# Attention stage of a six-stage image model: ScalarE's functions and the feature split one step back

## The chip, the cores and the metric

One core of a Trainium2 chip. The metric is the device time of one execution in microseconds, from three runs: 6,864.52 median, 6,858.64 lowest, 6,875.67 highest.

## The reference

32 images of 16 x 16 tokens with 192 channels pass through six stages: a Mamba block, a Fourier block, a determinantal attention (the change is here), a gated mixture of experts, attention over a small memory, a second mixture of experts. The attention, for each token i of each of 12 heads with 16 channels:

```python
sim = k @ q_i; sim = where(arange(T) <= i, sim, -inf)
_, top_idx = top_k(sim, 8)                     # 8 nearest earlier keys
for comb in (8 singles, 28 pairs):             # together with token i itself
    K, V = k[idx], v[idx]
    log_det = log(det(K @ K.T) + 1e-6)         # score = log_det / (2 or 3)
    out_s = softmax(K @ q_i / 4) @ V
probs = softmax(scores); y = probs @ outs      # then a projection, added to x
```

## The kernel before, in words

`dpp_attention_phase` works through the 32 images in 12 steps each; a step is two heads of one half (128 tokens) of the image, steps 0 to 5 the first half (128 keys), steps 6 to 11 the second (256 keys, two one-hots, twice the gather). Each engine runs a hand-written `body(n, u, i, back, last)` per step, `steps` (L2076) lays them out: image 0, then a loop whose body holds two images (an odd one, then an even one), then image 31, then one empty pass that drains the pipeline. An engine executes its queue in order, so the order of the calls in `body` is the order of the work; semaphores join the engines.

The path of a step's index, for step i:

- PE computes the scores (`score`, L2647), one step ahead.
- VectorE finds the 8 largest and their positions (L2529, L2536).
- ScalarE casts the positions (`cast_index`, L2205), PE turns them (L2659), ScalarE copies the result (`copy_turned`, L2213), SyncE writes it to HBM (L2137) and reads it back spread over 128 partitions (L2143).
- VectorE makes the one-hot from it in step i+2 (L2544).
- PE gathers keys, values and norms with it in step i+3 (L2678); ScalarE evacuates the two halves (`take_gathered`, L2222 to L2224).
- GpSimd multiplies key pairs (`products`, L2333 to L2339) in its step i+3; VectorE sums them to dots in step i+4 (L2553).

The rest of an image n is done in the steps of image n+1, by constants: VectorE's sim stage in step 0 (L2395 to L2400), denominators in 1 (L2408, L2410), gaps in 3 (L2420 to L2430), determinants in 4 (L2438 to L2451), scores in 5 (L2460 to L2464), rows in 6 (L2473 to L2482), alpha in 7; GpSimd's weighing (L2322) in 7 and 8, VectorE's sum of it in 8 and 9. Between two such stages ScalarE has one function: `differences` (Exp, L2237, step 0), `denominators` (Ln, L2241, step 1), `gaps` (Square, L2245, step 3), `logs` (Ln, L2249, step 4), `weights` (Exp, L2254, step 5). Each waits for VectorE's stage of its own step, and VectorE's stage of a later step waits for it. Within ScalarE's body the order is: `take_gathered` twice, `cast_index`, the function, then the front of the next image (`normalise`, `front`), last `copy_turned`.

The gather's operand `feat3` is the image's features in three bf16 pieces: ScalarE rounds (`split_high`, L2194), GpSimd subtracts (`split_rest`, L2309), ScalarE rounds the rest (`split_middle`, L2198), GpSimd subtracts again (`split_low`, L2314). In the kernel before, the first two are issued in step 11 of the image before, the last two in step 0 of the image. `keep_own` (L2232) copies the token's own value.

Of the kernel before, what the change touches and what calls it, by code (L numbers as in the profile page):

```python
# [15 lines left out]
B, HH, WW, C = 32, 16, 16, 192  # L16
# [10 lines left out]
def counted(n):  # L27


    return n + 1  # L30
# [1965 lines left out]
def dpp_attention_phase(nc, x_res, moments, consts, w):  # L1996

    with ExitStack() as ctx:
# [95 lines left out]
                body(B, 0, i, back, True)  # L2094

        SIMS, DENOM, GAP, DET, SCORE, ROWS, ALPHA, VALUE, OUT, PROJECT = 0, 1, 3, 4, 5, 6, 7, 8, 10, 11
        FRONT, NORMALISE, SQUARE, OWN, SPLIT = 3, 2, 10, 11, 11

        def whole(n):

# [2 lines left out]
        def previous(n, u, i, k):  # L2103

            return (n - 1, 1 - u) if i == k and (whole(n) or n > 0) else None

        def next_image(n, u, last):

            return None if last or (isinstance(n, int) and n == B) else (n + 1, 1 - u)
# [11 lines left out]
        with nc.Block() as block:  # L2121
# [27 lines left out]
            def _(act):  # L2149
# [42 lines left out]
                def split_high(n, u):  # L2192
                    act.wait_ge(S["own_ready"], counted(n + 1))
                    nc.scalar.copy(feat3[:, u, :, 0, :, :], feat[:, u, :, :, :]).then_inc(S["mid_ready"], 1)  # L2194

                def split_middle(n, u):
                    act.wait_ge(S["rest_ready"], counted(n + 1))
                    nc.scalar.copy(feat3[:, u, :, 1, :, :], rest_f[:, :, :, :]).then_inc(S["mid_ready"], 1)  # L2198

                def cast_index(n, u, i):  # L2200

                    q = count_of((n, u, i))
                    act.wait_ge(S["found_ready"], q * 2 + 2)
                    act.wait_ge(S["turned"], counted(q - 1) if not (isinstance(q, int) and q < 2) else 1)
                    nc.scalar.copy(index[:, i % 2, :, :], found[:, i % 2, :, :]).then_inc(S["index_ready"], 1)  # L2205
# [56 lines left out]
                def body(n, u, i, back, last):  # L2262
                    real, s3 = not (isinstance(n, int) and n == B), back(3)
                    if s3:
                        take_gathered(s3, 0)
                        take_gathered(s3, 1)
                    if real:
                        cast_index(n, u, i)
                    for k, do in ((SIMS, differences), (DENOM, denominators), (GAP, gaps), (DET, logs),
                                  (SCORE, weights), (OUT, out)):  # L2270
                        if previous(n, u, i, k):
                            do(*previous(n, u, i, k))
                    if i == 1 and not (isinstance(n, int) and n == B):
                        keep_own(n, u)
                    nxt = next_image(n, u, last)
                    if nxt and i == NORMALISE:
                        normalise(nc, xn[:, :, :], x_res, rstd, shift, nxt[0] * 2).then_inc(S["xn_ready"], 1)
                    if nxt and FRONT <= i < FRONT + 8:
                        front(*nxt, i - FRONT)
                    if nxt and i == SPLIT:  # L2280
                        split_high(*nxt)
                    if i == 0 and real:
                        split_middle(n, u)
                    if real:
                        copy_turned(n, u, i)

                normalise(nc, xn[:, :, :], x_res, rstd, shift, 0).then_inc(S["xn_ready"], 1)
                for k in range(8):
                    front(0, 0, k)
                split_high(0, 0)  # L2290
                steps(act, body)

            @block.gpsimd
            def _(pool):
# [12 lines left out]
                def split_rest(n, u):  # L2307
                    pool.wait_ge(S["mid_ready"], counted(n * 2 + 1))
                    nc.gpsimd.tensor_tensor(rest_f[:, :, :, :], feat[:, u, :, :, :], feat3[:, u, :, 0, :, :],  # L2309
                                            ALU.subtract).then_inc(S["rest_ready"], 1)  # L2310

                def split_low(n, u):
                    pool.wait_ge(S["mid_ready"], counted(n * 2 + 2))
                    nc.gpsimd.tensor_tensor(feat3[:, u, :, 2, :, :], rest_f[:, :, :, :], feat3[:, u, :, 1, :, :],  # L2314
                                            ALU.subtract).then_inc(S["split_ready"], 1)
# [27 lines left out]
                def body(n, u, i, back, last):  # L2343
                    if back(3):
                        products(back(3))
                    for t in range(2):
                        if previous(n, u, i, ALPHA + t):
                            weigh(*previous(n, u, i, ALPHA + t), t)
                    nxt = next_image(n, u, last)
                    if nxt and i == SQUARE:  # L2350
                        squares(*nxt)
                    if nxt and i == SPLIT:
                        split_rest(*nxt)
                    if i == 0 and not (isinstance(n, int) and n == B):
                        split_low(n, u)

                squares(0, 0)
                split_rest(0, 0)
                steps(pool, body)

            @block.vector
# [530 lines left out]
```

## Time and profile before

| | |
|---|---|
| median of three runs | 6,864.52 us |
| profiled execution | 6,853.56 us |
| its span | 6,851.9 us |
| mean granted TensorE clock | 0.731 of full speed |

The span is the time from the first to the last instruction of the profiled execution. A busy share is a mean over all six stages; the attention stage lies between about 1,580 and 4,350 us. An idle time is put down to what released the engine.

### The profile page before, as it was taken

How to read it: one execution, taken by the hardware profiler on the slowest of the kernel's cores; microseconds unless marked ns; L12 is line 12 of the kernel's file. 1: busy time of each engine (PE TensorE's matmuls, PEld its weight loads, DVE VectorE, ACT ScalarE, POOL GpSimd, SP SyncE). 2: the span in 40 equal slices, each digit the busy share in tenths (PEclk: the TensorE clock that was granted, in tenths of full speed). 3: DMA queues.
4: the chain of work that ended last, by engine and by line, in shares of the span. 5: the costliest groups of instructions: out<-in, count | busy, mean ns of one | idle time of the engine just before them, and what ended most of it. 6: DMA issues, size and time to landing. Idle time of an engine off the chain costs nothing. (4 is left out here: it accounts for less than half of the span.)

```text
span 6851.9 us, 140450 instructions
## 1 busy us (share of the span) xinstructions
PE 4985.4 (73%) x45364; PEld 3654.2 (53%) x45365; DVE 4293.3 (63%) x9002; ACT 2061.2 (30%) x6098; POOL 3267.7 (48%) x4341
## 2 busy tenths in 40 slices
PE   5777776987878888888888888334971997169990
PEld 2333333775555555555555555333850776069990
DVE  5777776227889989999899999723654333212223
ACT  3343333223333333333333333221210332123330
POOL 1222222115667777777777777334235000554447
PEclk8676777997666666666666666557985996589995
DMA  4000000002222222222222222212222002111113
GB/s 140 7 5 5 7 3 6 0 4 73 74 73 75 75 73 76 73 76 75 75 76 73 76 76 74 57 37 72 76 72 60 0 0 61 56 50 45 46 43 110
DMA packets 170739, 369.46 MB, mean 54 GB/s; under 512 B 35650, under 2 KB 100939, under 8 KB 169140
## 3 DMA queue, kind: packets, MB, share of 16 engines
q1 hardware_dynamic: 136404, 283.77, 12.6%
q0 software_dynamic: 33792, 78.69, 3.6%
q8 instruction: 312, 5.11, 0.3%
q14 instruction: 231, 1.89, 0.1%
HBM read 286.86 MB, written 75.50 MB: 53 GB/s over the span
## 5 line engine op out<-in xcount | busy, mean ns | idle before, releaser
L2333 POOL TENSOR_TENSOR l2a_prod<-l2a_keys 128x64 f32<-128x64 f32 (+1 forms) x2304 | 1143.7, 528 | 626.9 <-ACT l2a_norms L2224 619.7
L2678 PE MATMUL l2a_g<-l2a_feat,l2a_onehot 128*128 128x33 bf16 x27648 | 828.3, 187 | 49.4 <-DVE l2a_onehot L2544 24.8
L2678 PEld LDWEIGHTS l2a_g<-l2a_feat,l2a_onehot 128*128 128x128 bf16 x27648 | 807.2, 103 | 57.5 <-DVE l2a_onehot L2544 32.3
L2647 PE MATMUL l2a_s<-l2a_qkT 32*128 32x128 f32 (+1 forms) x1536 | 612.9, 489 | 53.3 <-issue 53.2
L2544 DVE TENSOR_SCALAR l2a_onehot<-l2a_spread,l2a_key_col 128x2048 bf16<-128x2048 bf16 x576 | 545.7, 974 | 141.4 <-DMA l2a_spread<-index_rows 105.1
L1734 POOL TENSOR_TENSOR l_hc<-l_hs,l_bc 128x512 f32<-128x512 f32 x192 | 243.1, 1266 | 794.2 <-DVE l_hs L1808 790.7
L2553 DVE TENSOR_REDUCE l2a_dots<-l2a_prod 128x72 f32<-128x1152 f32 x384 | 515.7, 1343 | 54.2 <-POOL l2a_prod L2339 54.2
L1903 PE MATMUL l_y<-l_hc,l_selT 128*96 128x512 f32 x384 | 308.2, 897 | 294.0 <-POOL l_hc L1734 294.0
L2596 PE MATMUL l2a_a<-l2a_tT,l2a_wqk 96*96 96x256 f32 x1024 | 408.9, 570 | 124.5 <-ACT l2a_tT L2175 124.5
L2222 ACT COPY l2a_keys<-l2a_g 128x128 f32<-128x128 f32 x768 | 199.7, 260 | 816.5 <-PE l2a_g L2678 800.5
L440 POOL DMA_INDIRECT rows_in<-l3f_dispatch_xn,l3f_dispatch_at x128 | 122.9, 960 | 652.5 <-ACT l3f_dispatch_xn L416 613.8
L652 POOL TENSOR_TENSOR l3f_w_own<-l3f_w,l3f_w_own 96x1536 fp32r<-96x1536 f32 x72 | 252.9, 3513 | 326.1 <-DVE l3f_w_own L753 326.1
L2647 PEld LDWEIGHTS l2a_s<-l2a_qkT 32*128 32x128 f32 x1536 | 304.5, 246 | 146.2 <-issue 91.8
L2596 PEld LDWEIGHTS l2a_a<-l2a_tT,l2a_wqk 96*96 96x96 f32 x1024 | 239.9, 248 | 222.0 <-ACT l2a_tT L2175 128.1
L695 PE MATMUL l3f_expert_h<-l3f_tT,l3f_w_own 96*128 96x256 f32 x2592 | 333.9, 288 | 8.9 <-POOL l3f_w_own L652 6.7
L695 PEld LDWEIGHTS l3f_expert_h<-l3f_tT,l3f_w_own 96*128 96x128 f32 x2592 | 320.6, 191 | 9.5 <-issue 7.1
L2339 POOL TENSOR_TENSOR l2a_prod<-l2a_keys,l2a_feat 128x256 f32<-128x256 f32 x384 | 319.9, 833 | 0.0
L759 DVE TENSOR_TENSOR l3f_tT<-l3f_expert_tp,l3f_tT 96x512 fp32r<-96x512 f32 x72 | 49.5, 687 | 421.7 <-ACT l3f_tT L726 421.7
L735 ACT ACTIVATE l3f_hT<-l3f_expert_h,l3f_b 128x256 f32<-128x256 f32 x432 | 181.0, 469 | 380.7 <-PE l3f_expert_h L695 380.7
L710 PE MATMUL l3f_expert_y<-l3f_w,l3f_hT 128*128 x1728 | 292.6, 326 | 0.0
L1808 DVE TENSOR_TENSOR_SCAN l_hs<-l_dA,l_state,l_dBu 128x512 f32<-128x512 f32 x192 | 261.9, 1364 | 39.4 <-ACT l_dA L1684 33.0
L710 PEld LDWEIGHTS l3f_expert_y<-l3f_w,l3f_hT 128*128 128x128 f32 x1728 | 279.1, 190 | 0.0
(403 smaller groups left out, 10979.3 us busy)
## 6 DMA issues: line engine op xcount, KB each, us to landing
l2a_spread<-index_rows SPq DMA_DIRECT2D x384, 512.0 KB, 3.7
rows_in<-main_zeros SPq DMA_DIRECT2D x1, 13824.0 KB, 59.4
l2f_xg<-rows_in SPq DMA_DIRECT2D x72, 192.0 KB, 2.4
rows_out<-l2f_ys POOLq DMA_DIRECT2D x72, 192.0 KB, 2.4
l3f_xg<-rows_in SPq DMA_DIRECT2D x72, 192.0 KB, 2.4
rows_out<-l3f_ys POOLq DMA_DIRECT2D x72, 192.0 KB, 2.4
l3f_w<-in_l3f_w SPq DMA_DIRECT2D x2, 4608.0 KB, 33.9
l_xT<-in_l_xT SPq DMA_DIRECT2D x16, 384.0 KB, 3.8
```

Of the source, the lines that this page charges most:

```text
L652: nc.gpsimd.tensor_tensor(w1_own[:, u, 1, :, :], w1[:, :, bass.ds(e, 1), :].rearrange("p h a f -> p h (a f)"), w1_own[:, u, 0, :, :].bitca ...
L695: ins = nc.tensor.matmul(h_ps[b][:, c % 2, :], w1_own[:, u, wp, h, c * P:(c + 1) * P], tT[:, u, tp_, h, :], start=h == 0 and wp == tp_, st ...
L710: ins = nc.tensor.matmul(y_ps[u][:, t * C:(t + 1) * C], hT[:, u, c, t * P:(t + 1) * P], w2[:, c, bass.ds(e, 1), :].rearrange("p a c -> p ( ...
L1808: nc.vector.tensor_tensor_scan(hs[:, g % 2, :], dA[:, g % 2, :], dBu[:, g % 2, :], state[:, 0, g:g + 1], ALU.mult, ALU.add).then_inc(scan_ ...
L1903: nc.tensor.matmul(y_ps[:, :], selT[:, g, :], hc[:, g % 2, :], start=g == 0, stop=g == G - 1).then_inc(hc_used, 1)
L2333: nc.gpsimd.tensor_tensor(made[:, j, at:at + wide * wide, :].rearrange("p (b a) f -> p b a f", b=wide), key[:, lo:lo + wide, :].unsqueeze( ...
L2339: nc.gpsimd.tensor_tensor(made[:, :, 0:8, :], both, feat[:, u, t, h:h + 4:3, 0:HS].unsqueeze(2).broadcast_to([P, 2, SLOTS, HS]), ALU.mult) ...
L2544: ins = nc.vector.tensor_scalar(onehot[:, s[2] % 2, kt, :, :].rearrange("p k t -> p (k t)"), spread[:, s[2] % 2, :, :].rearrange("p k t -> ...
L2553: nc.vector.tensor_reduce(dots[:, h:h + 4:3, :], prod[:, s[2] % 2, :, :, :], AX.X, ALU.add).then_inc(S["dots_ready"], 1)
L2596: ins = nc.tensor.matmul(o[0:HC, j * T:(j + 1) * T], wqk[:, h, 2 * (k - 1) + j, :], tT[0:HC, h, :], start=h == 0, stop=h == 1)
L2647: nc.tensor.matmul(o, qkT[rows, u, h // 3, t * P:(t + 1) * P], qkT[rows, u, 4 + h // 3, 0:nk], start=True, stop=False, skip_group_check=True)
L2678: ins = nc.tensor.matmul(g_ps[j][:, a * FEAT:(a + 1) * FEAT], onehot[:, s[2] % 2, kt, j * SLOTS + a, :], feat3[:, s[1], kt, piece, h, :], ...
```

## The change

The five functions of ScalarE are called one step later, with the same data, so that the stage of VectorE they wait for belongs to the step before; in `body` they stand where they stood, behind `cast_index`. `split_high` goes from step 11 (and from before the loop, for image 0) to step 0 of its own image, `split_middle` from step 0 to step 1, both now ahead of `copy_turned` and of the front's work. `keep_own` goes from step 1 to 2. GpSimd's `split_rest` goes from step 11 to 0 and `split_low` from 0 to 1, each behind the products of its step. VectorE's, PE's and SyncE's programs are unchanged.

```diff
-        FRONT, NORMALISE, SQUARE, OWN, SPLIT = 3, 2, 10, 11, 11
+        FRONT, NORMALISE, SQUARE, OWN = 3, 2, 10, 11
@@ ScalarE's body
                     if real:
                         cast_index(n, u, i)
-                    for k, do in ((SIMS, differences), (DENOM, denominators), (GAP, gaps), (DET, logs),
-                                  (SCORE, weights), (OUT, out)):
+                    for k, do in ((SIMS + 1, differences), (DENOM + 1, denominators), (GAP + 1, gaps),
+                                  (DET + 1, logs), (SCORE + 1, weights), (OUT, out)):
                         if previous(n, u, i, k):
                             do(*previous(n, u, i, k))
-                    if i == 1 and not (isinstance(n, int) and n == B):
+                    if i == 0 and real:
+                        split_high(n, u)
+                    if i == 1 and real:
+                        split_middle(n, u)
+                    if i == 2 and real:
                         keep_own(n, u)
...
-                    if nxt and i == SPLIT:
-                        split_high(*nxt)
-                    if i == 0 and real:
-                        split_middle(n, u)
                     if real:
                         copy_turned(n, u, i)
...
                 for k in range(8):
                     front(0, 0, k)
-                split_high(0, 0)
                 steps(act, body)
@@ GpSimd's body
-                    if nxt and i == SPLIT:
-                        split_rest(*nxt)
                     if i == 0 and not (isinstance(n, int) and n == B):
+                        split_rest(n, u)
+                    if i == 1 and not (isinstance(n, int) and n == B):
                         split_low(n, u)
 
                 squares(0, 0)
-                split_rest(0, 0)
                 steps(pool, body)
```

## Rows read from the trace of the kernel before

**Rows 1.** the page: busy time, share of the span and instructions by engine

```profile
PE 4985.4 (73%) x45364; PEld 3654.2 (53%) x45365; DVE 4293.3 (63%) x9002; ACT 2061.2 (30%) x6098; POOL 3267.7 (48%) x4341
```

**Rows 2.** busy time by stretch, 1,000 us of the attention stage, columns as named

```profile
1700.00:2700.00 1000.00, 815.05 (x11677) 586.14 (x11677) 908.27 (x1842) 341.33 (x1418) 716.67 (x1166) 0.66 0.22 74
```

**Rows 3.** waits, 1700 to 4200 us: in total, times, longest

```profile
ACT l2a_det L2249 <- DVEq L2452: 189.3, 28, 6.8
...
DVE l2a_onehot L2544 <- DMA l2a_spread<-index_rows: 85.3, 48, 4.5
...
DVE l2a_dots L2553 <- POOL l2a_prod L2339: 45.8, 33, 1.9
...
DVE l2a_onehot L2544 <- PE l2a_g L2678: 34.8, 21, 2.9
```

**Rows 4.** timeline, VectorE, image 12: start, length, engine, line, operation, [idle, releaser]

```profile
2619.40 1.10 DVE L2544 TENSOR_SCALAR l2a_onehot<-l2a_spread,l2a_key_col 128x2048 bf16<-128x2048 bf16 x1 [0.39 <-DMA l2a_spread<-index_rows]
...
2624.58 0.82 DVE L2544 TENSOR_SCALAR l2a_onehot<-l2a_spread,l2a_key_col 128x2048 bf16<-128x2048 bf16 x1 [1.81 <-DMA l2a_spread<-index_rows]
...
2628.86 1.05 DVE L2425 TENSOR_TENSOR l2a_gap<-l2a_ratio,l2a_dots 128x96 f32<-128x96 f32 x4
```

**Rows 5.** timeline, ScalarE, image 12

```profile
2612.06 1.08 ACT L2237 ACTIVATE l2a_ex<-l2a_ex 128x1056 f32<-128x1056 f32 x1 [5.73 <-DVE l2a_ex L2400]
2613.05 0.84 ACT L2198 CAST l2a_feat<-l2a_rest_f 128x792 bf16<-128x792 f32 x1
...
2619.37 0.25 ACT L2213 CAST l2a_indexT<-l2a_t 16x128 bf16<-16x128 f32 x1
```

**Rows 6.** timeline, GpSimd and VectorE, image 12, steps 0 and 1

```profile
2606.81 3.11 POOL L2333 TENSOR_TENSOR l2a_prod<-l2a_keys 128x64 f32<-128x64 f32 x6
...
2610.31 0.66 POOL L2339 TENSOR_TENSOR l2a_prod<-l2a_keys,l2a_feat 128x256 f32<-128x256 f32 x1
2613.96 1.94 POOL L2314 TENSOR_TENSOR l2a_feat<-l2a_rest_f,l2a_feat 128x792 bf16<-128x792 f32 x1 [2.99 <-ACT l2a_feat L2198]
...
2609.07 2.32 DVE L2397 TENSOR_TENSOR l2a_ex<-l2a_sims,l2a_top 128x96 f32<-128x96 f32 x4
```

**Rows 7.** timeline, GpSimd, image 13

```profile
2696.42 3.42 POOL L2333 TENSOR_TENSOR l2a_prod<-l2a_keys 128x64 f32<-128x64 f32 x6 [5.07 <-ACT l2a_norms L2224]
```

**Rows 8.** timeline, VectorE, image 13

```profile
2702.17 0.56 DVE L2408 TENSOR_TENSOR l2a_denom<-l2a_ex 128x192 f32<-128x192 f32 x1
...
2713.22 1.35 DVE L2553 TENSOR_REDUCE l2a_dots<-l2a_prod 128x72 f32<-128x1152 f32 x1
```

**Rows 9.** timeline, ScalarE, image 13

```profile
2702.22 0.23 ACT L2205 CAST l2a_index<-l2a_found 128x16 bf16<-128x16 uint32 x1
2702.47 1.28 ACT L2241 ACT_TABLE_LOAD   x1
2704.64 0.92 ACT L2241 ACTIVATE l2a_denom<-l2a_denom 128x864 f32<-128x864 f32 x1 [0.89 <-DVE l2a_denom L2410]
```

**Rows 10.** timeline, VectorE (and ScalarE's load), image 12, steps 5 and 6

```profile
2642.89 1.28 ACT L2254 ACT_TABLE_LOAD   x1
...
2647.39 0.76 DVE L2529 MAX8 l2a_sims<-l2a_s 128x8 f32<-128x256 f32 x2 [0.33 <-DVE l2a_det L2464]
...
2650.78 0.81 DVE L2473 TENSOR_REDUCE l2a_sums<-l2a_det 128x96 f32<-128x384 f32 x1
```

**Rows 11.** timeline, VectorE, then GpSimd, image 12, step 8

```profile
2663.01 3.10 DVE L2544 TENSOR_SCALAR l2a_onehot<-l2a_spread,l2a_key_col 128x2048 bf16<-128x2048 bf16 x2
...
2661.70 3.13 POOL L2322 TENSOR_TENSOR l2a_values<-l2a_values,l2a_alpha 128x1728 f32<-128x1728 f32 x1 [3.98 <-DVE l2a_alpha L2503]
```

**Rows 12.** timeline, GpSimd, then VectorE, image 14

```profile
2779.09 1.69 POOL L2309 TENSOR_TENSOR l2a_rest_f<-l2a_feat 128x792 f32<-128x792 f32 x1
...
2780.44 0.56 DVE L2395 TENSOR_TENSOR l2a_top<-l2a_sims,l2a_own 128x192 f32<-128x192 f32 x1
...
2798.14 1.34 DVE L2553 TENSOR_REDUCE l2a_dots<-l2a_prod 128x72 f32<-128x1152 f32 x1
```

## The prediction

> **What bounds the kernel now.** I read the page first for the share of each engine, then the attention stage's table by stretches, then its waits, then the timelines of a few images, engine by engine. No engine is full over the whole span [rows 1], and the page is no guide to this change, since it touches one stage, some 2,750 us long. There VectorE is busy 908 of 1,000 us, PE 815, GpSimd 717, ScalarE 341 [rows 2]. So VectorE sets the pace, and only its idle time can be given back, at most 9 per cent of the stage. The waits show where ScalarE stands: it sits 189 us before the Ln of the determinants alone, until VectorE has finished that very stage [rows 3]. While it sits, everything behind it in its queue waits: the copy of the turned index, hence SyncE's two DMAs, and the evacuation of the next gather, hence GpSimd's products. That is large in ScalarE's time, but what VectorE pays for it is in its own rows: 85 us for the DMA of the spread index, 35 us for PE's gather, 46 us for GpSimd's products, 166 us in 2,500 or 29 images [rows 3]. That is the ceiling of the change's gain, 5.7 us an image, about 180 us in all.
>
> The loop body holds two images. In the second one of a pair (image 12) VectorE waits 0.39 us at step 2 and 1.81 us at step 3, both for the index DMA [rows 4]. The chain behind the second: ScalarE reaches its Exp early, is idle 5.73 us until VectorE's sim stage ends, copies the turned index at 2619.37, and the one-hot starts 5.2 us later [rows 4, 5]. In the first of a pair (image 13) PE begins late after the loop's branch; GpSimd's products start only at 2696.42 and all follows from there [rows 7].
>
> **The change, part by part.** Nothing is added or removed: 5 activations, 3 splits and 1 own-value copy per image change place. DMAs: copy_turned of steps 0, 1, 3, 4 and 5 comes earlier, with SyncE's two transfers each; that of step 2 comes later, behind a table load, the Ln and the own-value copies. From there on five effects.
>
> (A) *The waits for the index DMA.* In image 12 copy_turned of step 1 would now follow at 2615.6: index found 2613.2, cast 0.2, Exp 1.08, split_middle 0.84, copy 0.25 [the durations: rows 5]. With the same 5.2 us the index is there at 2620.8, before VectorE asks. Both waits go, 0.39 and 1.81 us [rows 4].
>
> (B) *GpSimd's long subtractions move in front of other VectorE work.* This is what the diff doesn't show. In step 8 a pair of one-hots takes 3.10 us, where one alone takes 0.82 [rows 4]; it starts inside a GpSimd operation of 3.13 us and ends 1.28 us after it [rows 11]. A two-input operation is held too: L2395 in image 14 ends at 2781.00, 0.22 us after L2309 ended at 2780.78 [rows 12]. One-input reductions aren't. So each GpSimd operation holds a one-hot or a two-input operation of VectorE until its end. The Trainium skill says the same (GPSIMD Engine Reference, 8. Key points: GpSimd's interfaces to SBUF are shared, with contention against VectorE's two-input and two-port instructions), and it speaks against the change. Today split_rest (L2309, 1.69 us) and split_low (L2314, 1.94, after 2.99 us of idle) run before a step's products, while GpSimd has nothing else [rows 6, 12]. Afterwards each stands behind them, and they take 4.2 us from 2606.81 to the end of L2339 [rows 6]. Image 12: VectorE saves some 0.9 us (an estimate; step 8's pair loses 1.5) on the one-hots of step 0; products to 2609.1, then split_rest to 2610.8 in the middle of the sim stage (L2397), which waits; step 1 starts at 2612.2 instead of 2611.95. Its one-hot now meets products (+0.5). split_low starts at 2615.3 and holds L2408 to 2617.3; the denominators end 2618.7, not 2617.9. From there 1.0 search, 0.9 one-hot, 1.3 dots, 1.0 search, 0.9 one-hot: the one-hot of step 3 ends at 2623.9, now at 2625.40 [rows 4]. Gain of A and B together 1.5 us. Image 14, whose products are later, by the same count: split_rest at 2783.3 holds the sim stage's last operation, step 1 starts 1.2 us later, split_low costs 1.3 us more, the dots of step 3 start at 2797.6 instead of 2798.14 [rows 12]: gain 0.5. I take 0.8 for the second image of a pair; bounds -0.5 (a whole split more) and 2.7 (A with nothing lost).
>
> (C) *First image of a pair.* After 2696.42 GpSimd has, in its new order, products, split_rest, products, split_low, products: 4.5 + 1.7 + 4.4 + 1.9 + 4.1 = 16.6 us (products lie between 4.2 and 4.6, since L2333's six take 3.11 to 3.42 [rows 6, 7]), ending at 2713.0, and the dots need the last of them. They start at 2713.22 now [rows 7, 8]. So the wait for the index DMA in front of them is replaced by one for GpSimd. The Exp, behind the cast that came at 2702.22 [rows 9], ends at 2703.6, where VectorE wants it at 2702.17 [rows 8]: 1.4 us lost, but inside the time for which GpSimd holds the dots. Gain 0.2 here; images with a longer wait gain more; I take 0.5, bounds 0 and 2.
>
> (D) *The second Exp is exposed.* The weights move to step 6, behind the cast of the same step. Today the table load runs ahead of the wait, at 2642.89, and the Exp follows VectorE at once. In step 6 the search begins at 2647.39, its last index is out at 2648.95, the row stage starts at 2650.78 [rows 10]. New: cast to 2649.2, load 1.28 to 2650.5 [rows 9], Exp 0.92 to 2651.4 (the Ln over as many elements takes 0.92 [rows 9]): VectorE waits 0.65 us, in every image. Bounds 0.4 (one-hot itself held up) and 0.9. The other three are covered: the Square is done 4 us before its use; the Ln of step 2 is used in step 4; the Ln of step 5 ends some 0.6 us before the score stage. Without that cover each would cost up to its own length.
>
> (E) *Contention of the rest.* GpSimd's products of steps 0 and 1 no longer pause and cover the whole gap stage. Its four operations L2425 take 1.05 us with GpSimd idle; the like-shaped L2397 took 2.32 us beside products [rows 4, 6]. So +1.2 us there; in return GpSimd is idle when the det stage and the one-hots of steps 5 and 7 come, -0.9. I take +0.3 us an image; bounds -0.3 and +1.6.
>
> Sum over a pair: -0.8 - 0.5 + 2 x 0.65 + 2 x 0.3 = +0.6 us; 16 pairs +10 us. In the last, empty pass the Exp stands behind a gather's evacuation, an estimate of +2 us. Against the profiled execution (6,853.6 us, span 6,851.9) that makes 6,866; the median of the three runs is 10.9 us higher, which makes 6,876. I give 6,872. What a measurement of this kernel can tell from no change is about 0.3 per cent, 21 us; so the forecast is no change that can be seen, leaning to slower.
>
> **Rivals.** *The waits fall out whole.* GpSimd and VectorE overlap without new harm: pair -2.7 - 1.0 + 1.3 = -2.4 us, 38 us in all, 6,826. For it: VectorE's waits are real and the only idle time it has. Against: split_low is late in either order, and the measured holds of up to 3 us.
> *Contention decides.* Place: gap and det stage, sim and denominator stage of every image; price: E at its upper bound, 1.6 us an image, with A to D as taken: pair +3.2, 51 us, 6,915. It decides once GpSimd's products cover both stages, so once its idle before step 4 is gone and not given back in steps 4 and 5. For it: L2397's 2.32 us; against: GpSimd's total work is fixed.
> *A switch of tables costs more than its load.* If ScalarE stood still for as long again behind each load, D would be 1.28 us more an image: +41 us, 6,913. Row: in image 13 the load ends at 2703.75 and the Ln starts at 2704.64, as VectorE's operands arrive [rows 9]; so at most 0.89 us can hide there. The Trainium skill (ScalarE: Activation LUTs, What ACT_TABLE_LOAD costs) gives 1,283 ns for the load and some 1,380 ns of drain, 2.66 us a switch; the first agrees with the 1.28 us, the second would have to fit in 0.89, and doesn't.
> *It doesn't do what it says*: the evacuations wait for PE's gather anyway, as at 2696 in image 13. That is C, and the time is the forecast's.
>
> **Numbers.** Forecast 0.44, waits fall out 0.22, contention 0.28, table switch 0.06. Forecast cases come out faster 0.06, same 0.30, slower 0.08; the second gives 0.20 faster and 0.02 same; the third 0.26 slower and 0.02 same; the fourth is slower. Together faster 0.26, same 0.34, slower 0.40. The bounds of all terms at once give -56 and +77 us; the forecast's own range is 6,850 to 6,895; the range that reaches into both sides is 6,822 to 6,918.
>
> **What would show it.** Right: ScalarE's idle before L2249 near zero; VectorE's wait for the index DMA under 20 us; new rows of VectorE waiting for the Exp of L2254 (about 0.65 us, once an image) and L2237 (first image of a pair); L2425 longer, L2438 shorter; L2408 and L2397 ending 0.2 us after L2314 and L2309. Wrong: step 3 of the first image shorter by over 1 us, or no wait before L2473, or VectorE's busy time per image up by over 1.5 us.

## The result, and the profile after

The changed kernel takes 6,884.43 us (median of 19 runs, 6,862.67 to 6,917.17) against 6,863.42 us for the one before (19 runs, 6,846.64 to 6,876.10): ratio 1.0037, 95% interval 1.0025 to 1.0049. That is slower by 21 us, clear of the noise but small, 0.3 to 0.4 per cent; it lies 12 us above the forecast and inside its range. The profiled execution has a span of 6,890.3 us (6,851.9 before) at a mean clock of 0.727 (0.731).

The stage itself is best measured by VectorE's first and last search, 1585.8 to 4337.8 us before and 1602.0 to 4375.1 after: 2,752.0 and 2,773.1 us, +21.1. Another 16 us of the difference of the two profiled executions lie ahead of the stage and come from no edit: in the kernel of experiment 1, where nothing ahead of the stage is changed either, the first search is at 1602.2. From here on I use stage lengths, each from one profiled execution, and step lengths: a step runs from VectorE's first search (MAX8) in it to that of the next, as a mean over images 2 to 29; "even" is the second image of a loop body (as 12), "odd" the first (as 13). In `after` the lines of GpSimd are one lower, those of VectorE and PE two lower than before; in the kernels of the experiments they shift again, and the names of the tiles tell which operation is meant.

First the page's busy line, then the stretch of [rows 2]; the latter's columns are the stretch, its length, busy us of PE, weight loads, VectorE, ScalarE and GpSimd with instruction counts, the granted clock, DMA share and GB/s.

```profile
PE 5027.3 (73%) x45364; PEld 3684.9 (53%) x45365; DVE 4345.5 (63%) x9002; ACT 2088.3 (30%) x6098; POOL 3311.2 (48%) x4341
...
1700.00:2700.00 1000.00, 818.56 (x11595) 588.39 (x11595) 926.54 (x1841) 351.69 (x1425) 726.99 (x1161) 0.66 0.22 75
```

VectorE is busy 927 of 1,000 us, where it was 908 [rows 2], and the kernel is slower all the same: a VectorE operation that is held counts as busy. Its idle time was indeed given back, but the busy time grew by more. A share of busy time can't be read as work done here.

The waits of 1700 to 4200 us (line waited at, releaser, us in total, times, longest), against [rows 3]:

```profile
ACT l2a_keys L2222 <- PE l2a_g L2676: 961.6, 465, 8.8
ACT l2a_index L2205 <- DVE l2a_found L2534: 585.0, 227, 5.5
...
DVE l2a_dots L2551 <- POOL l2a_prod L2338: 65.0, 38, 1.9
...
DVE l2a_onehot L2542 <- PE l2a_g L2676: 38.4, 24, 3.2
...
DVE l2a_denom L2406 <- ACT l2a_ex L2237: 24.0, 14, 2.3
```

ScalarE's 189 us before L2249 [rows 3] are gone and so are the like waits before L2245 and L2254. It now sits before PE's gather and before the index instead, and no row of VectorE's waits for either. VectorE's 85 us for the index DMA [rows 3] have no row any more. New are the waits for the first Exp (24.0 us, 14 times, once in every odd image) and for the second (10.1 us in 29 images, a row of the groups below). The wait for GpSimd's products grew from 46 to 65 us.

The price is in VectorE's two-input operations. Groups by shape (line, engine, operation, tiles, shapes, count | busy us, mean ns of one | idle before it), first of before, then of after, each over 1700 to 4200 us:

```profile
L2438 DVE TENSOR_TENSOR l2a_det<-l2a_det,l2a_minor 128x96 f32<-128x96 f32 x84 | 37.6, 499 | 0.0
L2410 DVE TENSOR_TENSOR l2a_denom<-l2a_denom,l2a_ex 128x96 f32<-128x96 f32 x87 | 36.2, 468 | 1.0
...
L2425 DVE TENSOR_TENSOR l2a_gap<-l2a_ratio,l2a_dots 128x96 f32<-128x96 f32 x87 | 18.1, 262 | 0.0
```

```profile
L2542 DVE TENSOR_SCALAR l2a_onehot<-l2a_spread,l2a_key_col 128x2048 bf16<-128x2048 bf16 x511 | 513.4, 1031 | 38.4 <-PE l2a_g L2676 38.4
L2551 DVE TENSOR_REDUCE l2a_dots<-l2a_prod 128x72 f32<-128x1152 f32 x341 | 457.4, 1341 | 65.0 <-POOL l2a_prod L2338 65.0
...
L2408 DVE TENSOR_TENSOR l2a_denom<-l2a_denom,l2a_ex 128x96 f32<-128x96 f32 x84 | 54.5, 699 | 1.0
L2423 DVE TENSOR_TENSOR l2a_gap<-l2a_ratio,l2a_dots 128x96 f32<-128x96 f32 x84 | 40.8, 536 | 0.0
...
L2471 DVE TENSOR_REDUCE l2a_sums<-l2a_det 128x96 f32<-128x384 f32 x29 | 24.1, 830 | 10.1 <-ACT l2a_det L2254 10.1
...
L2436 DVE TENSOR_TENSOR l2a_det<-l2a_det,l2a_minor 128x96 f32<-128x96 f32 x84 | 16.2, 245 | 0.0
```

The same 96-element operation costs from 245 ns to 699 ns, by what GpSimd does beside it. The denominators (L2410, now L2408) went from 468 to 699, the gaps (L2425, now L2423) from 262 to 536, the determinants (L2438, now L2436) fell from 499 to 245. The reduction L2551, one input, is 1,341 ns in either kernel.

What that makes of a step shows in image 13. Three timelines of after (start, us, engine, line, operation; in brackets the idle time before it): VectorE, GpSimd, ScalarE.

```profile
2718.84 0.49 DVE L2527 MAX8 l2a_sims<-l2a_s 128x8 f32<-128x128 f32 x2
...
2725.96 1.35 DVE L2551 TENSOR_REDUCE l2a_dots<-l2a_prod 128x72 f32<-128x1152 f32 x1 [1.91 <-POOL l2a_prod L2338]
2729.59 0.69 DVE L2406 TENSOR_TENSOR l2a_denom<-l2a_ex 128x192 f32<-128x192 f32 x1 [2.27 <-ACT l2a_ex L2237]
2730.31 3.32 DVE L2408 TENSOR_TENSOR l2a_denom<-l2a_denom,l2a_ex 128x96 f32<-128x96 f32 x4
2733.56 0.48 DVE L2527 MAX8 l2a_sims<-l2a_s 128x8 f32<-128x128 f32 x2
...
2738.16 1.35 DVE L2551 TENSOR_REDUCE l2a_dots<-l2a_prod 128x72 f32<-128x1152 f32 x1
```

```profile
2721.49 3.42 POOL L2332 TENSOR_TENSOR l2a_prod<-l2a_keys 128x64 f32<-128x64 f32 x6 [5.96 <-ACT l2a_norms L2224]
...
2725.89 1.69 POOL L2308 TENSOR_TENSOR l2a_rest_f<-l2a_feat 128x792 f32<-128x792 f32 x1
...
2731.23 1.70 POOL L2313 TENSOR_TENSOR l2a_feat<-l2a_rest_f,l2a_feat 128x792 bf16<-128x792 f32 x1
...
2736.56 0.74 POOL L2338 TENSOR_TENSOR l2a_prod<-l2a_keys,l2a_feat 128x256 f32<-128x256 f32 x1
```

```profile
2728.45 1.10 ACT L2237 ACTIVATE l2a_ex<-l2a_ex 128x1056 f32<-128x1056 f32 x1
```

The step takes 14.72 us. VectorE waits 2.27 us for the Exp, which stands in ScalarE's queue behind both gather evacuations and the cast; then split_low (2731.23 to 2732.93) lies inside the four L2408, which take 3.32 us. In the kernel of experiment 1, where the same subtraction stands before the products of this step, the same step takes 11.12 us (2690.23 to 2701.35): the subtraction runs beside the reduction, which it doesn't hold, and the four L2410 take 1.71 us. VectorE, then GpSimd, of that kernel:

```profile
2695.37 1.35 DVE L2553 TENSOR_REDUCE l2a_dots<-l2a_prod 128x72 f32<-128x1152 f32 x1 [1.92 <-POOL l2a_prod L2339]
2699.00 0.69 DVE L2408 TENSOR_TENSOR l2a_denom<-l2a_ex 128x192 f32<-128x192 f32 x1 [2.27 <-ACT l2a_ex L2237]
2699.72 1.71 DVE L2410 TENSOR_TENSOR l2a_denom<-l2a_denom,l2a_ex 128x96 f32<-128x96 f32 x4
```

```profile
2695.30 1.70 POOL L2314 TENSOR_TENSOR l2a_feat<-l2a_rest_f,l2a_feat 128x792 bf16<-128x792 f32 x1
2696.95 2.52 POOL L2333 TENSOR_TENSOR l2a_prod<-l2a_keys 128x64 f32<-128x64 f32 x6
```

### The profile page after: what moved, and what is told of

It reads as the page before. It is cut to its first block and busy times, and to the rows that moved or that the text cites. A ratio compares the mean times of both kernels' runs of the same rounds, so it can differ in the third digit from the quotient of the medians.

```text
span 6890.3 us, 140435 instructions
## 1 busy us (share of the span) xinstructions
PE 5027.3 (73%) x45364; PEld 3684.9 (53%) x45365; DVE 4345.5 (63%) x9002; ACT 2088.3 (30%) x6098; POOL 3311.2 (48%) x4341
## 5 line engine op out<-in xcount | busy, mean ns | idle before, releaser
L2332 POOL TENSOR_TENSOR l2a_prod<-l2a_keys 128x64 f32<-128x64 f32 (+1 forms) x2304 | 1204.8, 555 | 576.4 <-ACT l2a_norms L2224 574.5
L2542 DVE TENSOR_SCALAR l2a_onehot<-l2a_spread,l2a_key_col 128x2048 bf16<-128x2048 bf16 x576 | 573.1, 1021 | 53.0 <-PE l2a_g L2676 39.4
L2551 DVE TENSOR_REDUCE l2a_dots<-l2a_prod 128x72 f32<-128x1152 f32 x384 | 515.1, 1342 | 73.3 <-POOL l2a_prod L2338 73.3
L2594 PE MATMUL l2a_a<-l2a_tT,l2a_wqk 96*96 96x256 f32 x1024 | 382.6, 540 | 0.7 <-ACT l2a_tT L2175 0.7
L2657 PE MATMUL l2a_t<-l2a_ident_bf,l2a_index 128*16 128x128 bf16 x384 | 95.6, 249 | 362.5 <-ACT l2a_index L2205 361.7
L2657 PEld LDWEIGHTS l2a_t<-l2a_ident_bf,l2a_index 128*16 128x16 bf16 x384 | 33.2, 86 | 515.3 <-ACT l2a_index L2205 487.0
L2338 POOL TENSOR_TENSOR l2a_prod<-l2a_keys,l2a_feat 128x256 f32<-128x256 f32 x384 | 291.2, 758 | 0.0
```

Of the source, the lines that this page charges most:

```text
L2332: nc.gpsimd.tensor_tensor(made[:, j, at:at + wide * wide, :].rearrange("p (b a) f -> p b a f", b=wide), key[:, lo:lo + wide, :].unsqueeze( ...
L2338: nc.gpsimd.tensor_tensor(made[:, :, 0:8, :], both, feat[:, u, t, h:h + 4:3, 0:HS].unsqueeze(2).broadcast_to([P, 2, SLOTS, HS]), ALU.mult) ...
L2542: ins = nc.vector.tensor_scalar(onehot[:, s[2] % 2, kt, :, :].rearrange("p k t -> p (k t)"), spread[:, s[2] % 2, :, :].rearrange("p k t -> ...
L2551: nc.vector.tensor_reduce(dots[:, h:h + 4:3, :], prod[:, s[2] % 2, :, :, :], AX.X, ALU.add).then_inc(S["dots_ready"], 1)
L2594: ins = nc.tensor.matmul(o[0:HC, j * T:(j + 1) * T], wqk[:, h, 2 * (k - 1) + j, :], tT[0:HC, h, :], start=h == 0, stop=h == 1)
```

## The experiments

Theory: the move of ScalarE's functions saves what VectorE waited for the index, and the move of GpSimd's two subtractions costs more than that. Rival: it is the new waits for the Exps that spend the gain. A second rival: not GpSimd's work, but ScalarE's new order does it. The ratios are of medians over several executions, the stage lengths of one execution each.

| | kernel | ratio to before, 95% interval | stage, us |
|---|---|---|---|
| | before | | 2,752.0 |
| | after | 1.0037 [1.0025, 1.0049] | 2,773.1 |
| 1 | functions only | 0.9936 [0.9921, 0.9951] | 2,703.0 |
| 2 | splits only | 1.0032 [1.0021, 1.0043] | 2,784.3 |
| 3 | after, Exps first | 1.0001 [0.9987, 1.0016] | 2,751.7 |
| 4 | after, subtractions in four | 1.0078 [1.0051, 1.0106] | 2,811.6 |
| 5 | 1, Exps first | 0.9925 [0.9912, 0.9939] | 2,705.2 |
| 6 | 1, second Exp first | 0.9961 [0.9944, 0.9978] | 2,711.6 |
| 7 | 1, split_middle and split_low a step later | 0.9941 [0.9923, 0.9959] | 2,731.8 |
| 8 | 5, split_low two steps later | 0.9943 [0.9929, 0.9957] | 2,735.7 |
| 9 | after, subtractions of one head | 0.9879 [0.9860, 0.9898] | 2,666.1 |
| 10 | 1, subtractions of one head | 0.9876 [0.9855, 0.9897] | 2,669.2 |
| 11 | 5, split_low ahead of the products | 0.9924 [0.9909, 0.9939] | 2,711.6 |
| 12 | 5, whole split in step 11 | 0.9925 [0.9908, 0.9941] | 2,712.0 |

**1, functions only.** The one line of the change in ScalarE's body with the five `+ 1`; the split and the own copy stay where they were.

> The kernel before with only the five functions one step later; the feature split (both engines) and keep_own stay where they were. Theory H (the loss sits in GpSimd's two subtractions, which now stand behind products and hold VectorE's two-input operations to their end): the waits for the index DMA go (85 us in 29 images before, none after) and steps 0 and 1 don't grow by 0.5 and 2.5 us an image as they did; the exposed Exps stay. About -1.3 us an image: 6,820 us, 6,800 to 6,845, ratio to before about 0.994. Rival R (the functions' own move makes it slower, by the exposed Exps and by products that cover the gap stage): not under 6,863, rather 6,885 as with the whole change.

6,818.57 us, stage -49 us, as expected: the function move alone is the gain that the prediction's rival "the waits fall out whole" had priced at 6,826. Its new waits are those of after:

```profile
DVE l2a_dots L2553 <- POOL l2a_prod L2339: 38.4, 24, 1.9
DVE l2a_denom L2408 <- ACT l2a_ex L2237: 24.4, 14, 2.3
DVE l2a_onehot L2544 <- PE l2a_g L2678: 17.9, 15, 2.5
...
DVE l2a_sums L2473 <- ACT l2a_det L2254: 9.6, 30, 0.4
```

But the move of ScalarE's functions also moves a subtraction that it doesn't touch. Since ScalarE no longer sits before its first Exp, `split_middle` comes early, and GpSimd's split_low, issued where it was, starts in even images 7.9 us after the image's first search, inside the sim stage, where before it started after 10.7 us, behind that stage. It holds L2398, an operation over 24 elements that took 0.22 us as a mean before. VectorE, then GpSimd, of kernel 1 in step 0 of image 12:

```profile
2607.45 1.67 DVE L2398 TENSOR_TENSOR l2a_lane<-l2a_sims,l2a_own 128x24 f32<-128x24 f32 x1
```

```profile
2607.08 2.01 POOL L2314 TENSOR_TENSOR l2a_feat<-l2a_rest_f,l2a_feat 128x792 bf16<-128x792 f32 x1
```

Step 0 of even images is 1.6 us longer in kernel 1 than before, as it is in after (1.5).

**2, splits only.** After, with the old line of the five functions.

> The whole change, but the five functions at their old steps: only the split on both engines and keep_own one step later. H: split_low now also waits for split_middle behind the Ln of step 1, and ends in step 2 or 3, in front of the products of step 11 that VectorE's dots wait for: +1 to +3 us an image, 6,895 to 6,960. R: the split's place is neutral, 6,860 to 6,870.

6,893.11 us, stage +32: the sign is right, the size just under what was expected. Alone the two moves give -49 and +32, together +21, not -17. So they harm each other by 38 us. Part of it shows in the denominators. With the functions at their old steps split_low starts in even images 16.8 us after the first search, long behind the denominators (from 12.4), and the four L2410 take 469 ns (the three of 96 elements) and 670 ns (the one of 384), as before; in after, where both moved, it starts after 15.9 us, beside the same operations (the first of their stage starts after 14.5), and they take 699 and 1,115.

**3, both Exps at the head of their steps in after** (they leave the list behind `cast_index`).

```diff
+                    for k, do in ((SIMS + 1, differences), (SCORE + 1, weights)):
+                        if previous(n, u, i, k):
+                            do(*previous(n, u, i, k))
                     if s3:
                         take_gathered(s3, 0)
```

> The whole change, but the two Exps (steps 1 and 6) stand at the head of their step, ahead of the evacuations and the cast. H: the wait of L2254 (0.35 us an image) and of L2237 (1.7 us in the first image of a pair) go, but in the first image GpSimd's chain holds the dots of step 3 anyway: -20 us against the whole change, 6,865 (6,855 to 6,880). R: both waits come back whole, 0.35 + 0.85 = 1.2 us an image, -38 us: 6,846.

6,870.26 us, inside what was expected. Both waits are gone, 24.0 + 10.1 = 34 us of waiting, and the stage is 21 us shorter. The wait for GpSimd grew from 65.0 to 83.2 us, since the odd images' chain of products was as late as before:

```profile
DVE l2a_dots L2553 <- POOL l2a_prod L2340: 83.2, 56, 2.3
DVE l2a_onehot L2544 <- PE l2a_g L2678: 32.3, 17, 2.8
```

**4, both subtractions cut in four,** to hold VectorE for shorter stretches (shown is `split_rest`; `split_low` is cut in the same way).

```diff
+                    for t, a in ((0, 0), (0, 6), (1, 0), (1, 6)):
+                        ins = nc.gpsimd.tensor_tensor(rest_f[:, t, a:a + 6, :], feat[:, u, t, a:a + 6, :],
+                                                      feat3[:, u, t, 0, a:a + 6, :], ALU.subtract)
```

> The whole change, but each of GpSimd's two subtractions is cut in four operations of a quarter of the elements. H (a VectorE operation is held to the end of the GpSimd operation, so by its length): the two operations L2408 and L2410 of step 1 (step 1 grew by 2.5 us) lose under 0.6 us at a hold instead of up to 1.7; GpSimd itself pays some 0.5 us more an image for three more starts each: -20 to -30 us against the whole change, 6,860. Rival (what counts is how much work GpSimd does beside VectorE, not how it is cut): 6,884 or, for the added starts, up to 6,900.

6,922.18 us where 6,860 was expected, a plain miss and the slowest of all. A quarter takes not a quarter of 1.70 us but 0.65, so each subtraction became 2.61 us. GpSimd's groups, and VectorE's wait for it:

```profile
L2316 POOL TENSOR_TENSOR l2a_feat<-l2a_rest_f,l2a_feat 128x198 bf16<-128x198 f32 x112 | 69.8, 652 | 0.0
L2309 POOL TENSOR_TENSOR l2a_rest_f<-l2a_feat 128x198 f32<-128x198 f32 x112 | 69.7, 653 | 0.0
```

```profile
DVE l2a_dots L2555 <- POOL l2a_prod L2342: 100.8, 57, 2.3
```

The extra 1.8 us of GpSimd an image came back as 1.2 us of stage an image (38.5 us over 32). That fits the rival, by which it is GpSimd's total length that counts, and not only the single hold.

**5, the Exps first in kernel 1** (the diff of 3, on 1).

> The kernel before with the five functions one step later (the split where it was), and the two Exps at the head of their steps. H: VectorE's waits for L2237 (24 us in 14 images) and L2254 (10 us in 30) go, and GpSimd's chain, without the subtractions in it, no longer takes the time back: 20 to 35 us under the kernel with the functions alone (6,819), so 6,785 to 6,800, ratio 0.990. Rival: the time comes back as a wait for the dots, as it did with the whole change and the Exps first (-14 us): 6,805 to 6,818.

6,815.57 us: the rival's figure. 34 us of waits left VectorE's rows, and nothing came of it: GpSimd is what VectorE meets next, 61.0 us in place of 38.4.

```profile
DVE l2a_dots L2555 <- POOL l2a_prod L2341: 61.0, 47, 2.0
```

**6, only the second Exp first in kernel 1.**

> As the kernel with the functions alone, but only the second Exp (weights, step 6) at the head of its step. H: its wait of 0.35 us an image goes, nothing follows from it: -10 us, 6,808. Rival (a table load costs more than its 1.28 us, by a standstill of about as long behind it): -10 us and up to 40 more, under 6,790.

The wait in step 6 went (0.35 us an image) and the stage did not get shorter; expected was 6,808, measured 6,837.45 (6,813 to 6,851), its profiled execution 6,811.8. It speaks against a table load that costs more than its length: that would have given under 6,790. Why this kernel's median lies 19 us above kernel 1's, with intervals that overlap, I can't say.

**7, split_middle and split_low one step later in kernel 1.**

> As the kernel with the functions alone, but split_middle and split_low in step 1 as in the whole change (split_high and split_rest stay in step 11). It halves the move of the split. H: split_low behind the products of step 1 holds the denominators, which cost most in the whole change (step 1 grew by 2.5 us), so most of the 66 us between the two kernels comes with it: 6,850 to 6,875. Rival: split_rest behind the products of step 0 is the dear one: 6,815 to 6,835.

6,832.37 us, the rival's figure, and the expectation missed. The hold came as expected: the three denominators of 96 elements take 952 ns each, 383 in kernel 1. But the time can hardly be told from kernel 1's (ratios 0.9941 and 0.9936, with intervals that overlap widely), and by the stage lengths of one execution each it is 29 us of the 70 between kernel 1 and after. So the larger part, 41 us by the stages and more by the ratios, comes only when split_rest, split_high and the own copy move too. A held operation is not paid in full where VectorE would have waited afterwards anyway.

**8, split_low in step 2, behind the products, in kernel 5.**

> The kernel with the functions one step later and the Exps first, and GpSimd's split_low in step 2, behind its products, where VectorE has searches, a one-hot and dots, and two-input operations only later. H: in the second image of a pair the sim stage isn't held any more (step 0 is 10.3 us there, 8.7 before): -1.6 us in every second image, +0.8 for a held one-hot in some: -10 to -25 us against the Exps first, 6,765 to 6,785. Rival (the hold of VectorE is not what makes step 0 long): no change against the Exps first, or slower since PE's gather of step 3 needs the split.

6,826.79 us where 6,765 to 6,785 was expected and kernel 5 has 6,815.57: missed. PE's gather of step 3 reads the low piece and now waits for it.

```profile
PE l2a_g L2680 <- POOL l2a_feat L2316: 73.1, 29, 3.2
```

**9 and 10, the subtractions over one head of twelve,** in after and in kernel 1. So far the cost was GpSimd's by inference; this pair asks whether it is ScalarE's new order instead. Shown is `split_rest`; `split_low` is cut down in the same way, and the buffers are zeroed once ahead of the stage. What both kernels leave out is the second and third piece of eleven heads.

```diff
-                    nc.gpsimd.tensor_tensor(rest_f[:, :, :, :], feat[:, u, :, :, :], feat3[:, u, :, 0, :, :],
+                    nc.gpsimd.tensor_tensor(rest_f[:, :, 0, :], feat[:, u, :, 0, :], feat3[:, u, :, 0, 0, :],
```

> The changed kernel, but GpSimd's two subtractions handle one head of twelve only (66 elements in place of 792; the other heads' second and third pieces stay zero or stale, which is left out of the computation). Order, waits and semaphores are all as in the changed kernel. The stage of the changed kernel was 2,773 us long, that with only the functions moved 2,703 us; the 70 us between them I put down to the length of the two subtractions in their late places (they hold VectorE's two-input operations and stand in front of the products). Theory: with subtractions of some 0.5 us the 70 us are gone, the stage comes out within 10 us of that of the sister kernel e10 (the same short subtractions in their old places), both at 2,670 to 2,700 us; time about 6,800. Rival: the 70 us come from ScalarE's and the semaphores' new order (rounding in step 0 and 1, own copy in step 2, ahead of the turned index), not from GpSimd's length; then this stage stays 40 us or more above that of e10, at 2,730 or more, time about 6,850.

> The kernel in which only the functions moved, with the same short subtractions in their old places (steps 11 and 0; the rest of the middle and low pieces is left out). Both theories expect the same here: a stage of 2,670 to 2,700 us, up to 30 us under the 2,703 of its full-length form, since 3.5 us an image less of GpSimd's time stands beside VectorE's sim stage; time about 6,795. It is the floor against which e9 is read.

GpSimd's groups of 9, then of 10:

```profile
L2308 POOL TENSOR_TENSOR l2a_rest_f<-l2a_feat 128x66 f32<-128x66 f32 x30 | 13.3, 445 | 0.0
L2313 POOL TENSOR_TENSOR l2a_feat<-l2a_rest_f,l2a_feat 128x66 bf16<-128x66 f32 x30 | 9.9, 330 | 0.0
```

```profile
L2309 POOL TENSOR_TENSOR l2a_rest_f<-l2a_feat 128x66 f32<-128x66 f32 x30 | 22.4, 747 | 4.8 <-ACT l2a_feat L2194 4.8
L2314 POOL TENSOR_TENSOR l2a_feat<-l2a_rest_f,l2a_feat 128x66 bf16<-128x66 f32 x30 | 14.3, 476 | 0.0
```

This settles it. 9 takes 6,783.05 us and 10 takes 6,777.46. With short subtractions the two orders are 3 us apart in the stage (2,666.1 and 2,669.2), with whole ones 70 (2,773.1 and 2,703.0). All of the 70 us hangs on the length of two GpSimd operations: in their late places that length costs 107 us of stage, in their old ones 34. ScalarE's new order costs nothing that can be seen. The second rival falls.

The denominators in 9, with everything in the order of after:

```profile
L2411 DVE TENSOR_TENSOR l2a_denom<-l2a_denom,l2a_ex 128x96 f32<-128x96 f32 x90 | 37.6, 469 | 1.0
```

They take what they took in the kernel before, 469 ns where after has 699. So the products beside them are not what made them longer; split_low is.

**11 and 12, better places for the split,** both on kernel 5: 11 has split_middle and split_low at the heads of step 0, 12 has the whole split in step 11.

GpSimd's part of 11:

```diff
+                    if i == 0 and not (isinstance(n, int) and n == B):
+                        split_low(n, u)
                     if back(3):
                         products(back(3))
```

> e5 (functions moved, Exps first, split in its old steps) with split_middle at the head of ScalarE's step 0, ahead of the gather's evacuation, and split_low at the head of GpSimd's step 0, ahead of the products: the subtraction runs while VectorE does searches and one-hots. Theory (a subtraction costs by the two-input operations that it holds and by the products that it delays; GpSimd waits for the gather there anyway): the sim stage is no longer held, the even image's step 0 falls from 10.3 towards 8.7 us, the stage from 2,705 to 2,680 to 2,690 us, time 6,795 to 6,805. Rival: the one-hots of step 0 are held instead, or the products come later and take the gain back: 6,812 to 6,825.

> e5 with all four parts of the split in step 11: split_middle directly behind split_high on ScalarE, split_low directly behind split_rest on GpSimd. Theory: the same as for e11 but the wait for ScalarE's rounding (0.84 us) stands on GpSimd, and ScalarE's copy of the turned index of step 11 waits some 3 us for GpSimd's first subtraction and its own rounding, which the spread index of step 11 (used in step 1) has room for: stage 2,675 to 2,695 us, time 6,790 to 6,810. Rival: the late copy shows as a wait of VectorE's one-hot of step 1 for the DMA, or GpSimd's products of step 0 start later: no gain on e5 or a loss, 6,815 to 6,835.

6,817.3 and 6,816.96 us, both the rival's figure. 11 didn't clear the sim stage: in even images split_low starts 6.4 us after the first search, inside the stage (from 5.7), and in odd ones it starts after 4.6 us and holds the stage's first operation (L2397 there, 895 ns as a mean where kernel 5 has 459). The one-hots, which the rival named, are as in kernel 5 (1,050 and 1,051 ns), and the dots wait 68.2 us for GpSimd. In 12 the index DMA is late again:

```profile
DVE l2a_onehot L2546 <- DMA l2a_spread<-index_rows: 40.4, 25, 3.4
DVE l2a_dots L2555 <- POOL l2a_prod L2341: 37.8, 29, 1.9
```

So 1, 5, 11 and 12 are one result, 0.6 to 0.8 per cent below before. Best is kernel 5, ratio 0.9925 [0.9912, 0.9939]; against after it is some 1.1 per cent (0.9925 / 1.0037).

## Why the prediction was right, and where its terms were not

The total held, and so did the signs of A, B, D and E; C's reason did not, and B was 2.1 us too small as a mean over the even images. That the errors of the other terms took most of B's back is luck. Change in step length, us an image:

| steps | even | odd |
|---|---|---|
| 0 and 1 | +3.75 | +2.29 |
| 2 and 3 | -1.64 | -1.46 |
| 4 and 5 | -1.29 | -1.17 |
| 6 | +0.40 | +0.56 |
| 7 | -0.43 | -0.07 |
| 8 to 11 | +0.16 | +0.20 |
| all | +0.97 | +0.35 |

Inside step 3 the gap stage's operations got longer by 1.6 us together (three L2425 of 96 elements by 0.274 each, the one of 384 by 0.49, the rest 0.3). That is E's, so steps 2 and 3 without it are 3.2 and 3.0 us shorter. By the prediction's terms, for a pair of images:

| term | predicted | measured, and how |
|---|---|---|
| A + B (even image) | -0.8 | +0.5: 3.75 - 3.2 |
| C (odd image) | -0.5 | -0.7: 2.29 - 3.0 |
| D | +1.3 | +1.0: 0.40 + 0.56 |
| E | +0.6 | +0.2: 2 x 1.6 - 1.29 - 1.17 - 0.43 - 0.07 |
| steps 8 to 11 | 0 | +0.4 |
| sum | +0.6 | +1.3 (from unrounded terms), sixteen pairs +21 |

**A, right in kind, too small.** In image 12 I had 2.2 us of index waits to remove. All of them went, in all images: 85.3 us to none, 2.9 an image as a mean and 2.4 in even ones. Steps 2 and 3, with cheaper one-hots and a shorter wait for PE's gather beside it, give 3.2.

**B, right in kind, the step that failed.** My count of "Gain of A and B together 1.5 us" in image 12, 0.8 as a mean, came to a loss of 0.5, at the edge of the bad bound that I had set. My two counts put the end of step 1 at 0.8 us (image 12) and 2.5 us (image 14) later, 1.65 as a mean; measured are 3.75. The holds end where I said: in image 12 L2406 ends at 2640.06, 0.22 us after split_low, as in [rows 12]. What I missed is in two places. In step 1 (+2.25) split_low holds more than L2408 of before: the four denominators L2410, too, pay 1.1 us an image by the groups above (3 x 0.231 + 0.445), 1.5 in even images, and the one-hots of that step 0.7, where I had 0.5. In step 0 (+1.50) VectorE waits longer than before for the products (0.6 to 1.4 us) and for PE's gather (0.1 to 0.5), a delay that I had at nothing; the saving on this step's one-hots came, 0.4 us where I had 0.9. Over the whole image a one-hot costs 1,031 ns in place of 980, 18 times an image, 0.9 us, but that isn't B's: kernel 1, with the subtractions in their old places, has 1,070. The section of the Trainium skill that the prediction named (GPSIMD Engine Reference, 8. Key points), by which GpSimd shares its SBUF interfaces with VectorE's two-input instructions, agrees in kind with these rows; it gives no size, and the size was the question.

**C, right in sum, wrong in its reason.** I held that the 1.4 us for which VectorE waits for the first Exp lie "inside the time for which GpSimd holds the dots", so that the two waits cover each other. In image 13 GpSimd's chain from 2721.49 ended at 2737.30, 15.8 us later (I had 16.6), and VectorE asked for it at 2738.16, without a wait. So the index wait fell out whole there too. As a mean over odd images it was 3.2 us in step 3, and a wait of 0.5 us for GpSimd stands in its place; the step is 1.17 us shorter, over the 1 us that I had named as a sign of being wrong; and the Exp's wait is not covered by anything: 24.0 us in 14 odd images, 1.7 each, on top of it the denominators held. A gain and a loss of some 3 and 2.3 us stand where I had argued for almost no movement.

**D, right, too dear.** The wait for the second Exp is in every image: 10.1 / 29 = 0.35 us, just below my lower bound of 0.4 and about half of the 0.65 that I took. The rest of step 6's +0.40 and +0.56 is longer operations. VectorE, then ScalarE, of after in step 6 of image 12:

```profile
2672.46 0.83 DVE L2471 TENSOR_REDUCE l2a_sums<-l2a_det 128x96 f32<-128x384 f32 x1 [0.43 <-ACT l2a_det L2254]
```

```profile
2670.21 1.28 ACT L2254 ACT_TABLE_LOAD   x1
2671.50 0.93 ACT L2254 ACTIVATE l2a_det<-l2a_det 128x864 f32<-128x864 f32 x1
```

The Exp follows the load by 0.01 us, ends at 2672.43, and VectorE goes on at 2672.46. The rival that a switch costs more than its load finds nothing here to support it. A page of the Trainium skill (ScalarE: Activation LUTs, What ACT_TABLE_LOAD costs) gives some 1,380 ns of drain with a load; none shows between load and Exp here.

**E, right in sum.** L2425 is 1.3 us longer (I had 1.2) and the like operations L2438 1.0 shorter, as said; 0.2 us a pair in place of 0.6. The one-hots of steps 5 and 7, which I had getting cheaper, got dearer: 0.73 to 1.21 us in step 5, 0.82 to 0.98 in step 7, as means of one.

Two of the three signs that I had named for being wrong were met: the odd step 3, and VectorE's busy time an image, 79.28 to 80.89 us, up by 1.6 where I had set 1.5. So contention had more of the truth than I gave it, though not as the rival "contention decides" told it: that one put the price on E, at 1.6 us an image, and E came to 0.1. The price was in the sim and denominator stages, by the two subtractions, whose length is worth 107 us of stage (after against experiment 9). And two moves were priced as one kernel: one of them is 0.6 per cent faster, the other 0.3 slower alone and 1.0 on top of the first.

Three slips of the prediction changed nothing. By its own bounds all terms at once give -72 and +88 us a kernel (16 pairs of -4.5 and of +5.5), where it says -56 and +77. It counts 3 splits that move, and the diff moves four operations, two on either engine. And it gives 6,872 between its two sums, 6,866 and 6,876, without a reason.

What stays open is how the 107 us, 3.3 an image, divide into VectorE's operations held and products late. Between 9 and after the denominators differ by 1.25 us an image (3 x 0.230 + 0.560), the one-hots by 0.5 (18 x 0.027) and the waits of the dots by 0.9 (65.0 and 38.1 us in 29 images); 0.7 I haven't placed. Which of these the 38 us belong to, by which the moves harm each other, no experiment separates.

## What to carry to other kernels

When a change moves work of several engines at once, price each engine's part as a kernel of its own and try them apart: here the part that was only there to clear ScalarE's queue worked, and the part that went with it ate the gain. Place a long GpSimd operation by what VectorE does beside it (reductions and searches take no harm, two-input operations and one-hots stand still), and look at it again after every change on another engine: the move of ScalarE's functions alone carried split_low into the sim stage. Whether it stands ahead of its engine's products or behind them made no difference here (experiments 5 and 11). When two waits are removed and the time doesn't move, look at the wait that grew: here the dots' wait for GpSimd, 38 to 61 us.

## What the runs showed of the hardware

- A short GpSimd subtraction is far from proportionally short: 66 elements a partition take 330 to 747 ns, 198 take 653, 792 take 1,701. Between the last two that is 1.76 ns an element and some 300 ns for each operation (by that line 66 elements would take 420, so it is rough). Cutting one in four costs 0.9 us.
- A VectorE operation that starts inside one of the two GpSimd subtractions ends after it, by a time that goes with its own size: two-input operations of 24 elements 0.04 us after, of 96 elements 0.11 to 0.12, of 192 elements 0.21 to 0.22, of 384 elements 0.41 to 0.42 (all such cases in before and after), one-hots 0.55 us after. The one-hots beside the weighing, whose operations take 3.1 us, end 0.55 us after it too, in before and in after alike. So the hold lasts to the end of GpSimd's operation, however long that is.
- It works the other way as well: a subtraction that starts while a one-hot runs takes longer. In the kernel before it takes 1.68 or 1.69 us in 32 cases and 1.94 us or more in the 32 others, and these are the ones that start inside a one-hot.
- A reduction over 1,152 elements takes 1,341 to 1,343 ns in before, after and kernel 1 alike, whatever GpSimd does beside it.
